# Writing out the engine loops of a four-layer gated cross-attention kernel

## The reference

```python
x = x + tanh(g_xattn[0]) * L0_xattn(layernorm(x), ctx, ...)   # single-head attention
x = x + tanh(g_ffn[0])   * L0_ffn(layernorm(x), ...)          # linear + routed LoRA, top 2 of 8
x = x + tanh(g_xattn[1]) * L1_xattn(layernorm(x), ctx, ...)   # windowed attention, window 16
x = x + tanh(g_ffn[1])   * L1_ffn(layernorm(x), ...)          # linear + LoRA mixed by a router
x = x + tanh(g_xattn[2]) * L2_xattn(layernorm(x), ctx, ...)   # low-rank attention, 16 heads
x = x + tanh(g_ffn[2])   * L2_ffn(layernorm(x), ...)          # sign weights, routed scales
x = x + tanh(g_xattn[3]) * L3_xattn(layernorm(x), ctx, ctx, pos, mask, ...)  # 32 heads, 8 KV, rope
x = x + tanh(g_ffn[3])   * L3_ffn(layernorm(x), ...)          # routed LoRA, top 2 of 4
```

## Time and profile before

| | us |
|---|---|
| median of 3 runs | 2311.14 (2310.07 to 2311.7) |
| the profiled execution | 2309.02 |
| its span, first to last instruction | 2307.3 |
| PE busy | 1930.9 (84%) |
| DVE busy | 1694.7 (73%) |
| ACT busy | 560.0 (24%) |
| POOL busy | 604.1 (26%) |
| mean granted TensorE clock | 0.894 |

### The profile page before, as it was taken

The page is one execution under the profiler, slowest core; times in us unless marked ns, Lnnn a source line. Parts: engine busy times, 40 slices in busy tenths (PEclk is TensorE's granted clock), DMA queues, the critical chain, the costliest instruction groups (busy, mean ns, idle before and its releaser), DMA issues. The chain is left out here.

```text
span 2307.3 us, 40366 instructions
## 1 busy us (share of the span) xinstructions
PE 1930.9 (84%) x14722; PEld 1103.7 (48%) x14872; DVE 1694.7 (73%) x3005; ACT 560.0 (24%) x1326; POOL 604.1 (26%) x728
## 2 busy tenths in 40 slices
PE   4488778887788777888775789999999999999876
PEld 3344456434564345643452345555455545555432
DVE  4379754896558965489653688888888888888875
ACT  3122223212232122321221212222222222222221
POOL 0210203102131021310210354444344434343210
PEclk7699877998779987899775999999999999999987
DMA  6447201572014720157004111212111111111101
GB/s 216 146 125 215 83 1 38 137 203 82 1 46 136 198 80 1 47 133 211 14 1 136 60 56 47 65 28 74 43 50 45 55 47 46 47 28 29 33 24 37
DMA packets 134607, 176.82 MB, mean 77 GB/s; under 512 B 46304, under 2 KB 73568, under 8 KB 134288
## 3 DMA queue, kind: packets, MB, share of 16 engines
q1 hardware_dynamic: 134416, 174.20, 25.5%
HBM read 132.09 MB, written 42.07 MB: 75 GB/s over the span
## 5 line engine op out<-in xcount | busy, mean ns | idle before, releaser
L1138 POOL TENSOR_TENSOR early_vare<-early_mv,w_eps 128x1 f32<-128x1 f32 x96 | 31.5, 328 | 839.6 <-DVE early_mv L1203 825.0
L350 PE MATMUL la_ps<-w_xTl,la_wqh 128*128 128x512 bf16 x512 | 197.2, 385 | 16.1 <-POOL la_wql L2084 8.0
L2079 POOL TENSOR_TENSOR la_q<-la_straight,la_rot 128x512 f32<-128x512 f32 x128 | 163.3, 1276 | 168.7 <-DVE la_rot L2143 168.7
L350 PE MATMUL la_ps<-la_wol,la_oTh 128*128 128x512 bf16 x512 | 199.7, 390 | 6.7 <-issue 0.2
L351 PE MATMUL la_ps<-la_woh,la_oTl 128*128 128x512 bf16 x512 | 199.5, 390 | 0.0
L349 PE MATMUL la_ps<-w_xTh,la_wqh 128*128 128x512 bf16 x504 | 195.0, 387 | 3.9 <-DVE la_rot L2143 3.8
L351 PE MATMUL la_ps<-w_xTh,la_wql 128*128 128x512 bf16 x510 | 195.9, 384 | 0.0
L752 PE MATMUL early_ps<-early_products,w_heads 128*32 128x512 f32 x1024 | 129.6, 629 | 63.1 <-DVE early_products L1354 32.0
L2092 POOL TENSOR_TENSOR la_p<-la_s,la_rec 128x256 f32<-128x256 f32 x128 | 93.0, 727 | 324.9 <-DVE la_rec L2164 324.9
L2025 ACT ACTIVATE la_oTh<-la_ps 128x256 bf16<-128x256 f32 x256 | 84.3, 381 | 301.7 <-PE la_ps L1936 301.7
L349 PE MATMUL la_ps<-la_woh,la_oTh 128*128 128x512 bf16 x392 | 153.1, 391 | 0.0
(11 more groups left out here) (329 smaller groups left out, 4725.0 us busy)
## 6 DMA issues: line engine op xcount, KB each, us to landing
early_vR<-scr_v SPq DMA_DIRECT2D x128, 257.0 KB, 5.2
early_wkv<-wkv SPq DMA_DIRECT2D x32, 512.0 KB, 4.4
la_v<-v SPq DMA_DIRECT2D x64, 256.0 KB, 3.8
k<-early_ctxt SPq DMA_DIRECT2D x32, 256.0 KB, 3.6
v<-early_ctxt SPq DMA_DIRECT2D x64, 128.0 KB, 2.8
scr_p<-early_weights SPq DMA_DIRECT2D x16, 512.0 KB, 2.7
early_pR<-scr_p SPq DMA_DIRECT2D x32, 256.0 KB, 3.4
w_raw_q<-in_Wq SPq DMA_DIRECT2D x8, 1024.0 KB, 6.7
```

The source lines that it names most:

```text
L350: pe.matmul(out, lh[c], rl[c], start=False, stop=False)
L2079: rope_sum.send(pool.tensor_tensor(dst, straight[:, slot, :], rot[:, slot, :], ALU.add))
```

## The change

All hardware loops become Python loops over numbers. The instructions of engines are the same and in the same order; what goes is the loops' own instructions, all register arithmetic, the registers in DMA addresses and waits, and the class `Apart`, so that every wait is on a constant. The loops of `prepare_last` and of SP in `last_attention` are written out as well. The program grows: PE's stream from 6,773 to 12,806 program instructions, DVE's from 2,315 to 3,319, ACT's from 896 to 1,419, POOL's from 740 to 977, SP's from 588 to 600.

```diff
-class Head:
...
-class Apart:
-    def __init__(self, eng, once, n):
-        self.eng, self.once, self.n = eng, once, n
-
-    def wait_ge(self, sem, value):
-        with self.eng.register() as held:
-            self.eng.reg_alu(held, value, 0, ALU.max)
-            self.eng.wait_ge(self.once, self.n)
-            self.eng.wait_ge(sem, held)
...
             def keep_kv(turn, f):
                 g = f // 2
-                banks.wait_drained(apart, turn, "kv", f)
+                banks.wait_drained(sp, turn, "kv", f)
...
-            with sp.Fori(0, TURNS - 1) as turn:
+            for turn in range(TURNS - 1):
                 attention1(turn)
...
-                    banks.wait_free(apart, turn, "out2", j, 0)
-                    banks.wait_free(apart, turn, "out2", j, 1)
+                    banks.wait_free(pe, turn, "out2", j, 0)
+                    banks.wait_free(pe, turn, "out2", j, 1)
...
             ahead(0)
-            with pe.Fori(0, TURNS - 1) as turn:
+            for turn in range(TURNS - 1):
                 body(turn, True)
             body(TURNS - 1, False)
...
                 def statistics(x, j):
                     n = st.step(dve.bn_stats(stats[:, j, :], x[:, j, :]))
-                    st.after(n, apart)
+                    st.after(n)
                     stats_ready.send(dve.bn_aggr(mv[:, j, :], stats[:, j, :]))
...
-            with pe.Fori(0, TURNS) as turn:
+            for turn in range(TURNS):
                 for k, step in enumerate(("cos", "sin")):
...
-        def heads(eng, head):
-            head(0, 0)
-            with eng.Fori(0, KV // 2 - 1) as pair:
-                head(Head(pair, 1), 1)
-                head(Head(pair, 2), 0)
-            head(KV - 1, 1)
+        def heads(head):
+            for turn in range(KV):
+                head(turn, turn % 2)
...
-            with sp.Fori(0, KV - 2) as turn:
+            for turn in range(KV - 2):
                 head(turn, True)
```

More of the change, by code:

```diff
@@ L556, in load_kv_weights @@
                 if g >= 2:
-                    banks.wait_filled(apart, turn, "kv", 2 * (g - 2) + 1)
+                    banks.wait_filled(sp, turn, "kv", 2 * (g - 2) + 1)
                 wkv_in[g % 2].send(sp.dma_start(
@@ L586, in shifted_values @@
             def shifted_values(turn, j):
-                banks.wait_filled(apart, turn, "sum1", j - 2)
+                banks.wait_filled(sp, turn, "sum1", j - 2)
                 load_values(sp, turn, j)
@@ L617, in attention1 @@
                 k_kept.wait(sp, turn, KV - 1)
[L618 removed]
+                v_kept.wait(sp, turn, KV - 1)
             def store(turn):
                 for j in range(QUAD):
[L622 removed]
+                    x_done.wait(sp, turn, j)
                     stored.send(sp.dma_start(io["x_mid"][bass.ts(turn * QUAD + j, P), :], xq[:, j, :]))
@@ L1125, in _ @@
             ahead(0, None)
-            with act.Fori(0, TURNS - 1) as turn:
+            for turn in range(TURNS - 1):
                 body(turn, True)
@@ L1180, in _ @@
             ahead(0)
-            with pool.Fori(0, TURNS - 1) as turn:
+            for turn in range(TURNS - 1):
                 body(turn, True)
@@ L1255, in body @@
                         n = own.step(dve.bn_stats(stats[:, j, :], xin[:, j, :]))
-                        own.after(n, apart)
+                        own.after(n)
                         stats_ready.send(dve.bn_aggr(mv[:, j, :], stats[:, j, :]))
@@ L1401, in body @@
                 logits(1, ("route", 1), R1, w["rb1"][:, :])
-                st.after(top(e1, 1), apart)
+                st.after(top(e1, 1))
                 for j in range(QUAD):
@@ L1499, in _ @@
             body(0, True, "lows")
-            with dve.Fori(0, TURNS - 1) as turn:
+            for turn in range(TURNS - 1):
                 body(turn, True)
@@ L1586, in _ @@
         def _(act):
-            with act.Fori(0, TURNS) as turn:
+            for turn in range(TURNS):
                 for k, step in enumerate(("cos", "sin")):
@@ L1966, in _ @@
             scores(0, ("score", "first"), 0, 0)
-            heads(pe, head)
+            heads(head)
         @block.scalar
@@ L2056, in _ @@
             exponentials(0, 0, 0)
-            heads(act, head)
+            heads(head)
         @block.gpsimd
@@ L2125, in _ @@
             divide(0, 0, 0)
-            heads(pool, head)
+            heads(head)
         @block.vector
@@ L2291, in _ @@
             softmax(0, Steps(dve, first_step, 2, 0), ("score", "first"), 0, 0, 0)
-            heads(dve, head)
+            heads(head)
 def build(nc, io):
```

29 lines of the change are left out of this document (8 added, 21 removed).

## The result

The changed kernel takes **2284.42 us** (median of four runs, 2283.28 to 2291.78), the kernel before 2310.61 us in the same comparison (2309.1 to 2311.7). The ratio is 0.9881, with a 95% interval of 0.9862 to 0.9901: 26.2 us or 1.2% faster. The forecast was 2283.7 us in a range of 2274 to 2297, and the forecast sum, 27.4 us, was nearly met as well. As the experiments show, that sum has one term right for a reason that was told too widely, and a remainder that came out near the truth because two errors cancelled. That the median lies within a microsecond of the forecast is luck: in two later comparisons the same change gained 23.8 and 23.2 us.

A forecast was written before the change was run, and what follows sets the result against it. PE was taken to bound the last attention, no engine alone the early layers. Terms 13.4 + 10.2 + 0.9 + 2.5 + 0.4 = 27.4 us, off the 2311.1 us median, gave 2283.7 us, range 2274 to 2297.

The forecast's parts named there:

- The back-edges of the loop of pairs: Last attention: writing out the loop over pairs of heads removes PE's idle time at its two jumps back, 13.4 us.
- the two stalls: Last attention, PE at the first jump back: idle 1.04 us, seven small matmuls, idle another 3.41 us, both by "issue".
- The early layers' back-edges: Early layers: PE's jumps back lie under queued matmuls and a wait for DVE, so removing them is worth 0.
- Waits on registers: Early layers, turns 0 to 2: constants instead of registers in waits gain 10.2 us, plus 0.9 us at turn ends.
- My own rival: Early layers give next to nothing, leaving 2297 us; chance 0.20, shared with the rival that the branch isn't the price.
- the 0.54 us wait at attention 0: Early layers, turn 1: DVE waits 0.54 us for PE; in turn 3 it doesn't, taken as support for the register term.
- `Apart`: Early layers: waits as instructions of their own delay DVE's statistics by 0.07 us each; removal gains 2.5 us, bounds 0 to 6.7.
- The whole early part: Everything forecast outside the last attention's jumps back, some 14 us.
- `prepare_last`: Preparation of the last layer: PE's branch costs 215 ns taken against 76 ns, three times; gain 0.4 us at most.
- Written-out code: Whole program: the longer code is read in order, ahead of need, so its added cost is 0.
- The rival "slower": PE's densest stretches: written-out code arrives late, 3.41 us per boundary; 2331 us at fourteen boundaries; chance 0.03.
- The 108 ns for a branch: Skill page's branch time: two jumps back worth 0.2 us, sum about 14 us; the prediction went by the trace instead.

The follow-up runs named there:

- the two with a loop back: Changed kernel with the last attention's loop of pairs put back, once for PE alone (2290.84 us), once for ACT, POOL, DVE and SP (2293.66 us).

## Why the prediction came out right, step by step

*The back-edges of the loop of pairs*, 13.4 us: right. Written out alone the last attention gives 14.7 us, and the rows of after show 6.77 us everywhere. What I told of the mechanism was incomplete. I took the two stalls as the price of a taken branch. The first one is; the second, and with it most of the price, comes only if the target lies just before a block's end. At another place the same two edges cost 3.7 us, and 9 to 10 of the 13.4 us were to be had without writing out anything. And I put the other engines' jumps at zero because they wait for PE. That holds only while PE's own stall is longer: with PE straight they cost 1.7 us at each edge.

*The early layers' back-edges*, 0: right, as far as the measurement reaches. The first matmul of turn 1 waits for DVE for as long as it did:

```profile
376.98 0.22 PE L349 MATMUL early_ps<-early_xTh,w_Mh 128*128 128x128 bf16 x1 [1.47 <-DVE early_xTl L1160]
```

*Waits on registers*, 10.2 + 0.9 us: wrong. The step that failed is "Turn 3 has the same operations and constants for its waits", used as a control. Turns 1 and 2, of equal code, differ by 7.8 us within one execution (235.3 and 243.1 in the run with `Apart` on DVE, where all turns are straight), and turn 3 by 4.7 between two (240.7 and 245.4), and the uncertainty of 1 us, read from turns 1 and 2, was far too small. My own rival said this ("Turn 3 could be quicker for another reason than its waits"); I gave it too little because two measures agreed that were one: the 0.54 us wait at attention 0 was part of the same chance. Measured: about nothing, where `Apart` stands as well.

*`Apart`*, 2.5 us in bounds of 0 to 6.7: the idle time on DVE came out to 6.6 us as worked out. What it costs is not settled. At the statistics alone it cost 2.0 us, near the 2.5, but no more than the measurement's reach; everywhere together 9.5 us, above the upper bound, which counted only statistics on DVE. SP and PE, put at 0, cost 1.9 us by themselves, again within that reach; in the trace PE's own wait at attention 2's last product is some 2 us longer with `Apart` (5.5 against 3.4).

*The whole early part* was put at 14.0 us. The comparisons give, each less the last attention's 13.4: 12.8 (26.2), 10.3 (23.8) and 9.8 us (23.2). The run with the early layers alone gives 20.7 - 9.7 = 11.0, the two with a loop back 23.3 - (13.4 - 2.0) = 11.9 and 20.5 - (13.4 - 3.4) = 10.5. So about **11 us** by the medians, and 8 by the stage's length in the profiles. The two terms' errors cancelled: 11 us of registers that weren't there stood in for `Apart` and for what else the written-out early layers gain. That is luck, not foresight. If `Apart` is worth less than that, the rest has no name yet.

*`prepare_last`*, 0.4 us: not seen; 78.7 us before and after, and 79.8 us in the further execution of after.

*Written-out code*, 0: right. PE's transfers went from 129 to 120, and in the last attention, where its instructions are densest, PE shows no idle time by "issue" before the scores or the weighted sums. The 3.4 us by "issue" in the early layers stand where before waited 5.0 us. The rival "slower" had its mechanism right, PE running dry at the end of a piece, and its place wrong: the runs show it behind a jump, while in the straight code of after no idle time of PE by "issue" is longer than 0.84 us.

*The 108 ns for a branch.* The Trainium skill, Advanced Engine Details and Errata, section Control Flow Timing, gives about 108 ns for a compare-and-branch; the runs show 79 to 83 ns for one that falls through and 3.3 to 3.5 us for PE's in the loop of pairs when it jumps. The measurement decides. Another page of the Trainium skill fits them: Runtime: NRT & Kernel Launch, section Instruction fetch mechanics, says that a taken branch whose target isn't in the current window forces a fetch of the target before execution goes on. The trace agrees: a transfer of PE's instructions starts 1.0 us after the branch of 3.4 us (1663.0 and 1664.0). And `prepare_last`'s short loop, whose branch takes 215 ns and not the thirty times 108 ns that I told of every taken branch, is the case where the target is still there: no transfer of PE's instructions starts between 1222 and 1317 us.

## What to carry to other kernels

Before writing a loop out, look at what its back-edge costs in the timeline: if PE stands twice at the head of the loop, moving the head by a few dozen instructions may give most of the gain (here 9 to 10 of 13.4 us), and any edit ahead of the loop may give or take it by accident. Don't take one turn, or one stage of one profile, as a control for another: run the unchanged kernel again first and see how far it differs from itself. A control that agrees with a theory in two places counts once, if both lie in the same stretch of the same execution.

## What was not expected of the hardware

- A taken branch on PE to code that has to be transferred again costs 3.3 to 3.5 us of the sequencer's time, mostly hidden (PE stands 0.8 to 1.5 us); if the target is some 12 to 15 instructions before the end of a 16 KB block, a second stall of 3.1 to 3.9 us follows which nothing hides, and the edge costs 6.0 to 8.0 us with the slower matmuls behind it.
- 40 instructions that do nothing made the kernel before 9.1 us faster.
- DVE's own jump leaves it idle for 2.2 to 2.4 us by "issue" and passes 0.9 to 1.7 us of that on to a straight or a shortly stalled PE, although the branch itself takes only 55 to 72 ns in the trace.
- Executions of after differ by 8 to 12 us within a group (2284.84 to 2296.73 in one). In its profiled executions the early layers, where PE's granted clock changes between its two levels some 70 times, differ by 7 us, and the middle of the last attention, where it stays at 1.00, by nothing (650.0 us for six heads each time).
